# Value products of a decoder layer's attention issued in pairs of key groups, with buffers given up for a third probabilities buffer

## The reference, cut to what matters

```python
x = x + self_attn(layernorm(x), W_qk, W_v, alibi_slope)       # one head, causal
# cross-attention, H = 16 heads, D = 16
q = (Q @ wq.T).reshape(B, S, H, D).transpose(0, 2, 1, 3)
k = (K @ wk.T).reshape(B, S, H, D).transpose(0, 2, 1, 3)       # K = V = ctx
v = (V @ wv.T).reshape(B, S, H, D).transpose(0, 2, 1, 3)
scores = jnp.einsum('bhqd,bhkd->bhqk', q, k) / jnp.sqrt(jnp.float32(D))
attn = jax.nn.softmax(scores, axis=-1)
out = jnp.einsum('bhqk,bhkd->bhqd', attn, v)
x = x + out.transpose(0, 2, 1, 3).reshape(B, S, E) @ wfc.T
x = x + ffn(layernorm(x), w_gate, w_gate_up, w_down)           # 8 experts, top 2
```

## Time and profile before

| What | Value |
|---|---|
| median of 3 runs | 1108.36 us (1106.62 to 1108.38) |
| span of the profiled execution | 1101.4 us |
| TensorE busy over the span | 1042.1 us, 95% |
| VectorE, ScalarE, GpSimd busy | 666.3, 654.7, 522.1 us |
| TensorE busy from 505 to 1090 us, the expert part | 581.9 of 585.0 us |
| TensorE busy from 460 to 480 us, in `before_last` | 15.6 of 20.0 us |

### The profile page before, as it was taken

One profiled execution on the slowest core, in us unless ns is written; L12 is line 12 of the kernel. 1 busy time (PEld: TensorE's weight loads), 2 busy tenths in 40 slices (PEclk: granted clock), 3 DMA queues, 4 the chain that ended last, 5 costly groups with the idle time before them and its releaser, 6 DMA issues.

```text
span 1101.4 us, 36849 instructions
## 1 busy us (share of the span) xinstructions
PE 1042.1 (95%) x12742; PEld 884.4 (80%) x12742; DVE 666.3 (60%) x2153; ACT 654.7 (59%) x1439; POOL 522.1 (47%) x563
## 2 busy tenths in 40 slices
PE   4789999999999999889999999999999999999996
PEld 2457677777777776548899999999999999999996
DVE  5667788888888887854564444444444444444443
ACT  6588889888888888664443443444344344344332
POOL 4756677777777777423352332324323323323322
PEclk9899999999999999999999999999999999999999
DMA  5754666666666663386222451294221221238211
GB/s 181 238 187 161 170 174 176 172 181 181 179 182 181 183 183 108 107 297 232 45 37 36 143 152 29 46 393 113 33 34 29 33 33 29 37 100 297 42 29 20
DMA packets 91943, 142.76 MB, mean 130 GB/s; under 512 B 21232, under 2 KB 69808, under 8 KB 88560
## 3 DMA queue, kind: packets, MB, share of 16 engines
q1 hardware_dynamic: 76062, 122.96, 35.8%
q0 software_dynamic: 15808, 19.09, 10.7%
q10 hardware_dynamic: 18, 0.01, 0.0%
HBM read 268.13 MB, written 43.47 MB: 283 GB/s over the span
## 4 chain that ended last, share of the span: by engine, by line
PE 83%; DVE 6%; SPq 3%; ACT 3%; issue 2%; DMA 2%; POOL 1%; DVEq 0%; ACTq 0%; POOLq 0%
PE front L2307 17%; PE t_ring L2307 17%; PE s_ring L2325 8%; PE pv L2325 8%; PE pv L2022 5%; PE s_ring L1989 5%; PE t_ring L2007 5%; PE front L1864 4%; PE s_ring L1851 2%; PE front L1873 2%; PE front L1922 2%; PE tail L1873 2%; DVE nmax L1284 2%; PE tail L1851 1%; PE front L1851 1%
## 5 line engine op out<-in xcount | busy, mean ns | idle before, releaser
L787 POOL DMA_INDIRECT out<-y_sb,place_i x71 | 112.3, 1582 | 316.9 <-DVE y_sb L1761 121.9
L2307 PE MATMUL front<-rows_hi,wgu_sb 128*128 128x128 f16 x2272 | 213.5, 219 | 1.6 <-DVE rows_lo L1736 1.6
L2307 PE MATMUL t_ring<-rows_hi,wgu_sb 128*128 128x128 f16 x2272 | 214.6, 220 | 0.0
L1284 DVE TENSOR_REDUCE nmax<-s_ring 128x2 f32<-128x512 f32 x256 | 167.5, 682 | 53.7 <-PE s_ring L1989 52.5
L2307 PE MATMUL t_ring<-rows_lo,wgu_sb 128*128 128x128 f16 x1136 | 198.6, 220 | 0.0
L2307 PE MATMUL front<-rows_lo,wgu_sb 128*128 128x128 f16 x1136 | 197.6, 219 | 0.0
L2307 PEld LDWEIGHTS front<-rows_hi,wgu_sb 128*128 128x128 f16 x2272 | 180.5, 98 | 4.1 <-DVE rows_lo L1736 2.1
L2307 PEld LDWEIGHTS t_ring<-rows_hi,wgu_sb 128*128 128x128 f16 x2272 | 181.3, 98 | 1.6
L954 ACT ACTIVATE probs_t<-t_ring,mask_bias 128x512 f32<-128x512 f32 x256 | 167.1, 705 | 22.4 <-PE t_ring L2007 20.3
L1144 ACT ACTIVATE silu_g<-t_ring 128x256 f32<-128x256 f32 x142 | 54.6, 385 | 167.8 <-PE t_ring L2307 167.8
L1792 DVE SCALAR_TENSOR_TENSOR act_t<-t_ring,silu_g 128x256 f32<-128x256 f32 x142 | 60.3, 425 | 152.2 <-ACT silu_g L1144 152.2
(11 more groups left out here) (248 smaller groups left out, 2100.6 us busy)
## 6 DMA issues: line engine op xcount, KB each, us to landing
wgu_sb<-gu_split SPq DMA_DIRECT2D x71, 2048.0 KB
wd_sb<-down_split SPq DMA_DIRECT2D x71, 1024.0 KB
w_piece<-in_w_gu SPq DMA_DIRECT2D x32, 512.0 KB, 6.4
gu_split<-w_halves SPq DMA_DIRECT2D x32, 512.0 KB, 3.8
w_piece<-in_w_down SPq DMA_DIRECT2D x16, 512.0 KB, 7.6
down_split<-w_halves SPq DMA_DIRECT2D x16, 512.0 KB, 5.2
x_in<-in_x SPq DMA_DIRECT2D x16, 256.0 KB
ctx_in<-in_ctx_t_in SPq DMA_DIRECT2D x16, 256.0 KB
```

Of the source, the lines that this page charges most:

```text
L787: nc.gpsimd.indirect_dma_start(out=out, out_offset=bass.IndirectOffsetOnAxis(ap=place_i[:, j:j + 1], axis=0), in_=y_sb[:, j], in_offset=No ...
L1284: nc.vector.tensor_reduce(nmax[:, n // HJ, :, n % HJ], s_ring[n % 2][:].rearrange("p (r k) -> p r k", r=2), AX.X, ALU.max, negate=True).th ...
L2307: o = nc.tensor.matmul(gu_ring[f][:, part * SLOT:(part + 1) * SLOT], wgu_sb[j][:, w, at:at + P], r[:, j % 2, c], start=(i == 0), stop=(i = ...
```

## The change

On TensorE the value products of groups 2i and 2i + 1 stand one behind the other, at the place of the second or a little around it. Since the exponentials of the even group now wait longer for their reader, `probs_t` gets a third buffer: odd groups use buffer 0, even ones 1 and 2 in turn. The room comes from two copies that are given up: `w_scaled` (`split_hi` now scales the piece in place) and `ctx_t` (the context is no longer scaled by 32, so that the loaded `ctx_in` itself serves the subtraction, and the products of k and v are scaled back by 1 / PSCALE alone). `o_nt` shares the place of `xn3_t`, the sixth split weight has a tile of its own, and `w_raw` lies in `probs_t`. Buffers are therefore held longer, and some waits change: SP's `load_pieces` waits for `piece_split`, `load_next` for `ctxt_lo`, and the first exponential for `w_lo`.

```diff
-        w_scaled = ab("w_scaled", [P, CHUNKS, CHUNK])
-        w_raw = w_scaled[:].rearrange(...)
-        ctx_t = ab("ctx_t", [P, NC, S])
-        w_split = ab("w_split", [P, 6, 2, NC, D], F16)
+        w_split = ab("w_split", [P, 5, 2, NC, D], F16)
+        w_fc = ab("w_fc", [P, 2, NC, D], F16)
-        probs_t = ab("probs_t", [P, 2, 2, 2, S])
+        probs_t = ab("probs_t", [P, 3, 2, 2, S])
+        w_raw = probs_t[:].rearrange(...)
-        o_nt = ab("o_nt", [P, NC, S])
+        o_nt = xn3_t
+        def probs_of(g):
+            return 0 if g % 2 else 1 + g // 2 % 2
...
             def load_pieces(b, k, p):
-                    sp.wait_ge(piece_hi, CHUNKS * (b - 1))
+                    sp.wait_ge(piece_split, CHUNKS * (b - 1))
             def load_next(n, p):
-                sp.wait_ge(ctxt_sb, n - 1)
+                sp.wait_ge(ctxt_lo, n - 1)
...
             def f_ctxt(n, p, u):
-                nc.scalar.activation(ctx_t[:], ctx_in[:, p], ACT.Copy, scale=XSCALE)
-                nc.scalar.activation(ctx_h[:, HI], ctx_in[:, p], ACT.Copy, scale=XSCALE).then_inc(ctxt_sb, 1)
+                nc.scalar.activation(ctx_h[:, HI], ctx_in[:, p], ACT.Copy).then_inc(ctxt_sb, 1)
...
             def h_exp(b, g, r):
                 act.wait_ge(st_ps, 16 * b + 2 * g + r + 1)
-                if r == 0 and (not isinstance(b, int) or b > 0 or g >= 2):
-                    act.wait_ge(pv_ps, 8 * b + g - 1)
-                elif r == 0 and g == 0:
+                first = isinstance(b, int) and b == 0
+                if r == 0 and first and g == 0:
                     act.wait_ge(mask_set, 1)
+                    act.wait_ge(w_lo, 6)
+                elif r == 0 and g % 2 == 0 and not (first and g == 2):
+                    act.wait_ge(pv_ps, HJ * b + g - 3)
+                elif r == 0 and g % 2 == 1 and not (first and g == 1):
+                    act.wait_ge(pv_ps, HJ * b + g - 1)
...
             def split_hi(k, i, p, u):
-                if isinstance(k, int) and k == 0:
-                    act.wait_ge(w_lo, 2 * i + 2)
-                elif i == 0:
+                if i == 0 and not (isinstance(k, int) and k == 0):
...
-                nc.scalar.activation(w_scaled[:, i], w_piece[:, p, i], ACT.Copy, scale=WSCALE).then_inc(piece_hi, 1)
+                nc.scalar.activation(w_piece[:, p, i], w_piece[:, p, i], ACT.Copy, scale=WSCALE).then_inc(piece_hi, 1)
...
             def iteration(b, p, h, c, t, s, f, n):      # TensorE
-                    h_values(b, p, 0)                     # before f_v1
                     f_v1(b + 2)
...
+                    h_values(b, p, 0)
                     h_values(b, p, 1)
...
-                    h_values(b, p, 2)
                     t_xn3t(b - 1, q)
+                    h_values(b, p, 2)
                     h_values(b, p, 3)
...
                     h_scores_t(b, p, 5, 1)
-                    h_values(b, p, 4)
                     h_scores_t(b, p, 6, 0)
...
                     h_scores_t(b, p, 6, 1)
+                    h_values(b, p, 4)
                     h_values(b, p, 5)
...
                     f_xn2t(b + 2)
-                    h_values(b, p, 6)
                     h_scores(b + 1, q, h + p, 14, 15)
+                    h_values(b, p, 6)
                     h_values(b, p, 7)
```

More of the change, by code:

```diff
@@ L193, in decoder_layer @@
         w_piece = ab("w_piece", [P, 2, CHUNKS, CHUNK])
-        w_scaled = ab("w_scaled", [P, CHUNKS, CHUNK])
         w_halves = ab("w_halves", [P, CHUNKS, 2, CHUNK], F16)
-        w_raw = w_scaled[:].rearrange("p i c -> p (i c)")[:, 0:6 * NC * D].rearrange("p (i c n) -> p i c n", i=6, c=NC)
+        x_in = ab("x_in", [P, 2, NT, D])
+        ctx_in = ab("ctx_in", [P, 2, NC, S])
+        xn_h = ab("xn_h", [P, 2, NC, S], F16)
+        ctx_h = ab("ctx_h", [P, 2, NC, S], F16)
         fill_i = ab("fill_i", [P, ENTRIES // P], I32)
@@ L238, in decoder_layer @@
         o_n = ab("o_n", [P, NT, D])
-        o_nt = ab("o_nt", [P, NC, S])
+        xn3_t = ab("xn3_t", [P, NC, S])
+        o_nt = xn3_t
         xn3 = ab("xn3", [P, 2, NT, D])
-        xn3_t = ab("xn3_t", [P, NC, S])
         attention.close()
@@ L678, in rest, with ctx_rest, split_lo @@
                 pool.wait_ge(ready, n + 1)
-                nc.gpsimd.tensor_tensor(halves[:, LO], src[:], halves[:, HI], ALU.subtract).then_inc(lo, 1)
+                nc.gpsimd.tensor_tensor(halves[:, LO], src, halves[:, HI], ALU.subtract).then_inc(lo, 1)
             def xn_rest(n):
-                rest(xn_t, xn_h, xnt_sb, xnt_lo, n)
-            def ctx_rest(n):
-                rest(ctx_t, ctx_h, ctxt_sb, ctxt_lo, n)
+                rest(xn_t[:], xn_h, xnt_sb, xnt_lo, n)
+            def ctx_rest(n, p):
+                rest(ctx_in[:, p], ctx_h, ctxt_sb, ctxt_lo, n)
             def xn2_rest(n):
-                rest(xn2_t, xn2_h, xn2t_sb, xn2t_lo, n)
+                rest(xn2_t[:], xn2_h, xn2t_sb, xn2t_lo, n)
             def out_rest(c):
-                rest(o_nt, o_nh, ont_sb, ont_lo, c)
-            def split_lo(k, i):
+                rest(o_nt[:], o_nh, ont_sb, ont_lo, c)
+            def split_lo(k, i, p):
                 pool.wait_ge(piece_hi, CHUNKS * k + i + 1)
@@ L882, in weight_hi @@
                 act.wait_ge(raw_loaded[i], 16)
-                nc.scalar.activation(w_split[:, i, HI], w_raw[:, i], ACT.Copy, scale=PSCALE).then_inc(w_hi, 1)
+                nc.scalar.activation(split_of(i)[:, HI], w_raw[:, i], ACT.Copy, scale=PSCALE).then_inc(w_hi, 1)
             weight_hi(WQK)
@@ L933, in f_k @@
                     act.wait_ge(k_stacked[q], 16 * K_STACKS * u)
-                nc.scalar.activation(k_hi[:], as_chunks(bank_b(n)), ACT.Copy, scale=UNSCALE).then_inc(khi_sb, 1)
+                nc.scalar.activation(k_hi[:], as_chunks(bank_b(n)), ACT.Copy, scale=UNSCALE_W).then_inc(khi_sb, 1)
             def f_v2(n, p):
@@ L1873, in project @@
                         o = nc.tensor.matmul(bank_[:, t * D:(t + 1) * D], src[:, r, c, t * P:(t + 1) * P],
-                                             w_split[:, w, a, c], start=(start and i == 0 and c == 0),
+                                             split_of(w)[:, a, c], start=(start and i == 0 and c == 0),
                                              stop=(stop and i == len(products) - 1 and c == NC - 1))
@@ L2207, in before_last @@
                 h_scores(b + 1, q, h + p, 0, 2)
-                h_values(b, p, 0)
                 t_fc_rest(b - 1)
@@ L2374, in last_attention @@
                     h_scores_t(b, 1, g, 1)
-                    if g > 0:
+                    if g in (2, 4, 6):
+                        h_values(b, 1, g - 2)
                         h_values(b, 1, g - 1)
@@ L2393, in last_attention @@
                         t_gate(b - 1)
+                h_values(b, 1, HJ - 2)
                 h_values(b, 1, HJ - 1)
```

56 lines of the change are left out of this document (27 added, 29 removed).

## The result

| | median us (range), runs | an iteration | profiled span |
|---|---|---|---|
| before | 1106.99 (1103.88 to 1108.38), 6 | 28.15 | 1101.4 |
| changed | 1114.09 (1111.24 to 1116.93), 6 | 28.83 | 1115.2 |

The ratio is 1.006, 95% interval 1.0042 to 1.0078: slower by 7.1 us, above the 1112.5 at which the predicted range ended. The 1108.36 that the prediction started from is the median of three of the six runs of before.

A forecast was written before the change was run, and what follows sets the result against it. It took TensorE and ScalarE, both near their limit in the attention loop, as the bound. Loop 0, start -0.8 and end -0.8 made -1.6 on the 1101.4 span; with 7.0 carried over, 1106.8 us, range 1101.5 to 1112.5.

The forecast's parts named there:

- step 4: Loop, f_k: without ctx_t its wait for ctx_h (3.3 us in 8 waits) goes, saving 0.2 an iteration.
- rival D: Slower by VectorE, 8%: gprob falls behind the start of GpSimd's xn2_rest, last maxima late, +0.5 an iteration, 1114.
- The sign that was to tell C from D: Iteration over 28.4: scores(0) waiting for a DMA means rival C, transposes of the maxima waiting for VectorE rival D.
- rival C: Slower by SP's queue, 20%: 0.32 slack missing or q_lo's transfer landing late; without slack +0.45 an iteration, 1113.
- Offer: Value groups on TensorE: each pair saves 0.24, 55 pairs 13.2 us, if TensorE alone decided.
- steps 1 and 2: Loop up to t_gate: TensorE waits 0.5 at f_probs_t; exp(3,0) is 0.21 late, t_gate moves to T + 17.91.
- Step 3: Loop, t_gate to last maxima: pair 6/7 moves f_q by +0.40, cover 0.30, transposes of the maxima +0.10.
- Step 5: SP's stacking queue in the loop: scoresT(7,1) comes 0.64 later, the circle to scores(0) takes 28.2 to 28.3.
- Start: Before the loop: split_hi no longer waits 0.77 for weight pieces in a shared buffer, -0.8.
- End: Last two special batches: before_last +1.05, last_attention -1.8, sum -0.8, between -2 and +1.
- The 7.0: Difference between profiled span 1101.4 and median time 1108.36, carried over unchanged.
- The sum: Loop 0, start -0.8, end -0.8: -1.6 us in all, bounds -4.5 to +2.3.

The follow-up runs named there:

- e6: The kernel before with ctx_t given up and VectorE's cast of the positions (pos_i) moved ahead of q_lo; ratio 1.0008, iteration 28.16 us.
- e10: e6 with pair 6/7 alone in the loop, values(6) moved behind scores(14); ratio 0.9949, iteration 27.83 us.
- e9: e7 with pair 4/5 undone too, so only pairs 2/3 and 6/7 stay in the loop; ratio 0.9959, iteration 28.01 us.
- e7: e1 with pair 0/1 undone in the loop, values(0) ahead of f_v1 again; ratio 0.9996, iteration 28.12 us.
- e1: The changed kernel with VectorE's cast of the positions (pos_i) moved ahead of q_lo; ratio 1.0006 to the kernel before, iteration 28.33 us.
- e4: The changed kernel with the value groups in the order of the kernel before, buffers and copies as changed; ratio 1.0031, iteration 28.47 us.
- e2: The kernel before with only ctx_t given up; ratio 1.0027, iteration 28.48 us.
- e12: e1 with pair 4/5 undone in the loop, the other three pairs kept; ratio 0.9990, iteration 28.19 us.
- e11: The kernel before with pair 6/7 alone in the loop, values(6) moved behind scores(14); 1101.24 us beside 1105.88, ratio 0.9955.
- e3: The changed kernel with ctx_t put back, so both context copies; ratio 1.0011 to the kernel before, iteration 28.31 us.
- e8: e1 with pair 6/7 undone in the loop, values(6) ahead of scores(14) again; ratio 1.0077, iteration 28.79 us.
- e16: The kernel before with gprob and top_v moved behind the maxima of scores 15 on VectorE; ratio 0.9992, iteration 28.09 us.

## Why the prediction was wrong

The mean iteration, put together from the runs, one edit at a time:

| step | from, to | us |
|---|---|---|
| ctx_t given up, cast out of the way | before, e6 | +0.01 |
| pair 6/7 | e6, e10 | -0.34 |
| pair 2/3, with the new buffers | e10, e9 | +0.19 |
| pair 4/5 | e9, e7 | +0.11 |
| pair 0/1 | e7, e1 | +0.21 |
| the collision at the cast | e1, changed | +0.50 |

They add up from 28.15 to 28.83. The shares depend on the order: on top of the collision the four pairs are worth +0.37 (e4 to changed), without it +0.17.

**The step that failed is step 4**, "Without ctx_t, which took the same 0.6 as its twin, this wait goes, 0.2 an iteration". The wait did go. But it was smaller to begin with, 1.3 us in ten iterations of the loop, as one of the 8 waits in the earlier trace rows took 1.3 alone and lies outside this stretch; even that was not to be had (e6: q_lo takes ctx_h's place); and I did not ask what an earlier ctx_h sets off: ctx_rest, on GpSimd, 0.43 behind a small VectorE instruction that TensorE's t_ont waits for. Cost +0.50 (e1) with the pairs, +0.32 (e6 to e2) without. It is the mechanism of rival D, which I had looked for at gprob only and given 8%; at gprob the forecast of 0.2 came true (0.17). That D's 1114 is the measured time is luck. The sign that was to tell C from D, a wait at scores(0) or at the transposes of the maxima, pointed at neither: the wait is at t_ont.

**Offer, steps 1 and 2**: right in mechanism. The 16-matmul groups follow at 1.00 (247.73 to 248.73). The 0.09 is lost only in front of a group, though: 8 matmuls more take 1.00 - 0.58 = 0.42, so a group alone, with 0.58 to the next work, loses 0.16 behind it, and 0.09 + 0.16 is the 0.24 of a pair within rounding. TensorE waits 0.20 at f_probs_t (forecast 0.5, with ScalarE itself now 0.46 late from t_ont). exp(3,0) is late, and 0.46 is waited for at scoresT(6,0). t_gate starts at T + 18.37, forecast 17.91 plus the 0.46 of the cast. e7 and e12 correct one link: the wait at scoresT(6,0) comes from values(4), gone from in front of it, not from exp(3,0).

**Step 3** had the pairs at +0.10 together, about -0.03 for the first three and +0.13 for pair 6/7; they are +0.17 (the four pair rows of the table). The near agreement is luck, since both parts are wrong. Undersized was the loss from pairs 0/1, 2/3 and 4/5, +0.51; and the sign of pair 6/7 was wrong. It was priced by its delay of f_q, +0.40, less the cover of 0.30. What I missed is that the pair also brings scores(14), its maxima, gprob and the one-hot choice forward: TensorE's 0.30 in front of the last maxima and an idle 0.32 in front of the transposes of o_t, both in the iteration of the earlier trace rows, are gone in e11. Rival D had gprob's gain in view and set it at nothing, "VectorE gains 0.9 that TensorE doesn't need". How much of the pair's worth is gprob stays open.

**Step 5**, SP's queue, did not hold the steady loop: scores(0) waits for nothing there. It isn't far off: in the shorter iterations of e7, e9 and e12 scores(0) waits for q_lo's transfer in four or five of ten, by up to 0.4 (in e10 and e11 once at most). In changed something like rival C is seen twice in the run. In iteration 3 TensorE waited for q_lo's transfer 1.0 us (scores(0) starts 4.9 behind its issue), 0.5 before, and in before_last 1.4 where it was 0.4; there the profile names no releaser, but scores(0) starts 3.4 behind the issue of q_lo in changed and 3.2 before, about as long as such a transfer took in the earlier trace rows (waits of TensorE, changed, 100 to 147 and 445 to 495 us, then before, 445 to 495):

```profile
PE s_ring L1996 <- DMA q_stack<-q_lo: 1.0, 1, 1.0
...
PE s_ring L1996 <- issue: 1.4, 1, 1.4
```

```profile
PE s_ring L1989 <- issue: 0.4, 1, 0.4
```

**Start**, forecast -0.8: nothing. The first transposes of the maxima start at 58.08 at the earliest in a profile with the changed start (e12) and at 58.13 with the former one. The +3.4 of the profile of changed is that execution's: e11, whose start is that of the kernel before, has 61.99.

**End.** before_last, forecast +1.05: +3.1 in that profile, 1.0 of it at scores(0). From 468 to 472 us TensorE was busy 1.7 of 4.0; behind that the clock was at the lower level of 1.2 GHz for a while, the row of the window showing a mean of 0.57, and the eight matmuls of t_fc_rest took 1.70 to the next start, 0.89 before:

```profile
472.00:476.00 4.00, 4.00 (x30) 2.50 (x31) 2.50 (x8) 1.18 (x2) 0.96 (x1) 0.57 0.11 20
```

That leaves 1.3 for the pairs, by single profiles; the means over all profiles with and without them, 26.9 and 25.3, differ by 1.6. last_attention, forecast -1.8: the rest of the span is 621.4 to 622.1 in the six of e1 to e12 that have its pairs (e1, e3, e7, e8, e9, e12), 624.0 to 625.2 in the other six, so -3: the term was right in sign and too small. The profile of changed hides it (624.2); it lost 1.5 in the expert part, where TensorE was busy 35.9 of 40 us (551 to 591) and 37.5 in the same stretch of before (537 to 577).

**The sum.** -3 at the end, +1.3 to +3 in before_last and +7.6 in the loop make +6 to +8, where the medians differ by 7.1. I had -1.6, and about +2.3 at the outside. The profiles differ by 13.8 because they are not typical of their kernels: in every run whose span is on record the time is 1.7 to 1.8 us more than the span, so the span of 1101.4 belongs to an execution of about 1103.2 (an estimate from that difference) and the span of 1115.2 to the slowest run of changed, 1116.93. The 7.0 that stands ahead and in the prediction as what the times hold beyond the span is mostly this; as it was carried over unchanged, it cost the forecast nothing.

## What to carry to other kernels

When an instruction on a lightly used engine gets its input earlier, list what runs on its neighbour in the new place of its start, the very small instructions too: a cast of four elements was worth 6 us here (0.50 in each of twelve iterations). Regrouping work on a full engine pays only where the moved piece did not stand in a gap that exists anyway; keep such a piece in front of the wait, and test the pieces one by one, since in the loop one pair of four held all of the gain and the others only loss. Give a prediction for a change of several parts a term of its own for each part, with its sign open.

## What the runs showed of the hardware

A VectorE cast of 128x4 that starts 0.08 to 0.36 us behind a GpSimd subtraction of 128x512 (1.16 us) takes 1.10 to 0.82 us in place of 0.16 to 0.17, and ends with it (changed, e2, e4); gprob, 128x16, takes 1.08 or 1.10 where it starts 0.1 behind xn2_rest (before, e8) and 0.58 where it starts 0.6 behind (e16). Behind a stretch in which TensorE was busy 1.7 of 4.0 us the granted clock fell to a mean of 0.57 over 4 us (changed, 472 to 476 us). The first transposes of the maxima start anywhere between 58.1 and 62.0 us in the 19 profiles, whichever start the kernel has; a difference of a few us between two single profiles is to be split by stage before it is explained.
